# A two-layer vision tower on one core: setup and first token stage merged, first image load issued later, parameter preparations moved from VectorE to GpSimd

## The reference, cut to what matters

```python
h = tok(x, W)                                  # patches of 16 steps, real FFT, linear layer: (4, 1024, 64)
h = h + attn0(layernorm(h), wq, wkv, wo, ...)  # 16 heads, window of 128, rope, rms norm of q and k
h = h + moe0(layernorm(h), router, w1, b1, w2, b2)          # 8 experts, top 2
h = h + attn1(layernorm(h), Wq, bq, Wk, bk, Wv, bv, Wl, bl, gamma, beta)
h = h + ffn1(layernorm(h), gate_w, gate_b, w1, b1, w2, b2)  # 8 experts, top 1, limited capacity
```

## Time and profile before

| | us |
|---|---|
| median of 3 runs | 907.2 |
| lowest and highest | 906.09, 912.73 |
| profiled execution, its own time | 915.43 |
| its span in the profile | 913.3 |

### The profile page before, as it was taken

How to read it: one execution, slowest core, us unless ns; L and a number is a source line. 1 busy time by engine, 2 the same in 40 slices (tenths; PEclk the granted TensorE clock), 3 DMA queues, 4 the chain that set the end, 5 groups by cost and what they waited for, 6 DMA issues and landing times. The chain is left out here.

```text
span 913.3 us, 21178 instructions
## 1 busy us (share of the span) xinstructions
PE 734.4 (80%) x8200; PEld 481.4 (53%) x8200; DVE 611.8 (67%) x1233; ACT 449.5 (49%) x1405; POOL 411.8 (45%) x530
## 2 busy tenths in 40 slices
PE   4689999899998989988699979978899976306850
PEld 4343777435774447764277734764577753304640
DVE  0378887598885888875868836666577758504751
ACT  0022999237994359972389925212666631202000
POOL 0036666274662556643656612762033320571755
PEclk9999999999999999999979999988999987557755
DMA  8235000080000720001200000008000012117000
GB/s 294 73 137 136 2 3 3 19 247 11 3 3 1 224 50 3 4 2 27 64 2 3 3 1 1 2 2 117 1 2 3 2 53 76 36 43 121 15 11 14
DMA packets 60008, 41.30 MB, mean 45 GB/s; under 512 B 51760, under 2 KB 57389, under 8 KB 59124
## 3 DMA queue, kind: packets, MB, share of 16 engines
q1 hardware_dynamic: 57462, 33.03, 14.6%
q10 hardware_dynamic: 144, 4.19, 1.2%
q0 software_dynamic: 2304, 2.74, 0.9%
HBM read 25.44 MB, written 7.15 MB: 36 GB/s over the span
## 5 line engine op out<-in xcount | busy, mean ns | idle before, releaser
L797 ACT ACTIVATE work<-ps,small,rq 128x160 f32<-128x160 f32 x512 | 243.1, 487 | 32.7 <-DVE small L743 32.1
L776 POOL TENSOR_TENSOR work<-work,small 128x512 f32<-128x512 f32 x128 | 133.3, 1042 | 124.2 <-DVE small L760 124.2
L740 DVE TENSOR_REDUCE ps<-ps 128x4 f32<-128x640 f32 x128 | 106.6, 832 | 42.6 <-PE ps L650 41.0
L797 ACT ACTIVATION_READ_ACCUMULATOR work<-ps,small,rq 128x1 f32 x512 | 105.2, 205 | 0.0
L650 PE MATMUL ps<-kT,big 64*128 64x160 f32 x1024 | 99.1, 314 | 0.0
L752 DVE COPY pT<-ps 128x640 f32<-128x640 f32 x116 | 95.6, 824 | 0.3 <-issue 0.3
L685 PE MATMUL ps<-pT,vwin 128*64 128x128 f32 x1024 | 84.6, 283 | 9.9 <-ACT big L785 2.4
L270 PE MATMUL ps<-xT,s_proj_w 64*128 64x512 f32 x288 | 77.2, 653 | 12.1 <-PEq L213 7.0
L610 POOL TENSOR_TENSOR big<-prod 128x1024 f32<-128x1024 f32 x28 | 65.8, 2363 | 25.8 <-DVE prod L577 25.7
L650 PEld LDWEIGHTS ps<-kT,big 64*128 64x128 f32 x1024 | 77.1, 193 | 0.1
L685 PEld LDWEIGHTS ps<-pT,vwin 128*64 128x64 f32 x1024 | 57.0, 136 | 23.8 <-issue 20.1
(11 more groups left out here) (280 smaller groups left out, 1376.1 us busy)
## 6 DMA issues: line engine op xcount, KB each, us to landing
xb<-in_x SPq DMA_DIRECT2D x3, 4096.0 KB, 13.0
xb<-in_x ACTq DMA_DIRECT2D x1, 4096.0 KB, 15.2
vrem<-hl SPq DMA_DIRECT2D x64, 64.0 KB, 2.1
sent_rows<-empty_row SPq DMA_DIRECT2D x8, 325.0 KB
s_proj_w<-in_proj_w SPq DMA_DIRECT2D x1, 1536.0 KB, 6.2
big<-sent_rows SPq DMA_DIRECT2D x5, 264.0 KB, 5.1
big<-sent_rows SPq DMA_DIRECT2D x5, 256.0 KB, 4.6
xb<-in_ffn_w SPq DMA_DIRECT2D x1, 1028.0 KB, 4.7
```

The costliest lines, as they stand in the source:

```text
L740: ch.step(v.tensor_reduce(row_max(c), ps[:, s_banks(c), 0:2 * SPAN].rearrange("p e (h k) -> p e h k", h=2), X, ALU.max))
L776: g.tensor_tensor(probs[:, c % 3, :, 0:P], probs[:, c % 3, :, 0:P], bc(small[:, c % 4, 3, :], P), ALU.mult)
L797: nc.scalar.activation(probs[:, c % 3, q, :], bank[2 * (c % 2) + e][:, SPAN * hh:SPAN * hh + SPAN], ACT.Exp, bias=small[:, c % 4, 1, q:q + ...
```

## The change

The stages `setup` and `tokens` become one. ACT waits for `tok_loaded` before it issues the image load. All preparations, and three of the memsets, go from DVE to GpSimd, each as a chained step. DVE is left with four constants, `kT` and `empty_row`, the copy of the filters, then the layernorm, and `vbias` and `wvl` last. TensorE makes filters, token products, waits for `set_ready`, turns the tokens, waits for `bvrep` (`high_done`), makes the two small products (now in bank 7), then 4 instead of 6 idle products, and turns the normed tokens. On GpSimd the operations with a scalar per partition become tensor operations with a broadcast operand: `split_bias` has 9 instructions in place of 7.

```diff
-        def split_bias(v, ch, b, parts, high, low, rest):
-            ch.step(v.tensor_copy(high, b))
-            ch.step(v.tensor_tensor(rest, b, high, ALU.subtract))
-            ch.step(v.tensor_copy(low, rest))
-            ch.step(v.tensor_tensor(rest, rest, low, ALU.subtract))
-            ch.step(v.tensor_scalar(rest, rest, part_of[:, 2:3], None, ALU.mult))
-            ch.step(v.scalar_tensor_tensor(out=rest, in0=low, scalar=part_of[:, 1:2], in1=rest, op0=ALU.mult, op1=ALU.add))
-            ch.step(v.scalar_tensor_tensor(out=parts, in0=high, scalar=part_of[:, 0:1], in1=rest, op0=ALU.mult,
-                                           op1=ALU.add))
+        def split_bias(g, ch, b, parts, high, low, rest, chosen):
+            def of_part(k):
+                return part_of[:, k:k + 1].to_broadcast([P, E * D])
+            ch.step(g.tensor_copy(high, b))
+            ch.step(g.tensor_tensor(rest, b, high, ALU.subtract))
+            ch.step(g.tensor_copy(low, rest))
+            ch.step(g.tensor_tensor(rest, rest, low, ALU.subtract))
+            ch.step(g.tensor_tensor(rest, rest, of_part(2), ALU.mult))
+            ch.step(g.tensor_tensor(chosen, low, of_part(1), ALU.mult))
+            ch.step(g.tensor_tensor(rest, rest, chosen, ALU.add))
+            ch.step(g.tensor_tensor(chosen, high, of_part(0), ALU.mult))
+            ch.step(g.tensor_tensor(parts, rest, chosen, ALU.add))
...
+            @block.gpsimd
+            def _(g):
+                ch = Chain(g, S["pool_chain"])
+                ch.step(g.memset(zeros[:], 0.0))
+                ch.step(g.memset(row_of_t[:], 0.0))
+                ch.step(g.memset(window_mask[:], 0.0))
+                g.wait_ge(S["set_ready"], 1)
+                ch.step(g.tensor_tensor(bvrep[:], zeros[0:D, :], bvcol[:].to_broadcast([D, P]), ALU.add))
+                g.sem_inc(S["high_done"], 1)
+                for half in range(2):
+                    r = slice(D * half, D * half + CHUNK)
+                    ch.step(g.tensor_copy(row_of_t[r], row_of_t_rows[r]))
+                    ch.step(g.tensor_copy(window_mask[r], window_mask_rows[r]))
+                ch.step(g.tensor_scalar(bq[:], bq[:], 1.0 / D, None, ALU.mult))
+                ch.step(g.tensor_tensor(wqk[:], qn[:], kn[:], ALU.mult))
+                ch.step(g.tensor_scalar(wqk[:], wqk[:], float(np.sqrt(D)), None, ALU.mult))
+                ch.step(g.tensor_copy(moe_w2[:], sbuf["moe_w2"]))
+                ch.step(g.tensor_tensor(both_halves[:], ident[:, 0:D], ident[:, D:P], ALU.add))
+                ch.step(g.tensor_tensor(part_of[:, 0:3], ident[:, 0:3], ident[:, D:D + 3], ALU.add))
+                ch.step(g.tensor_tensor(part_of[:, 3:4], part_of[:, 0:1], part_of[:, 1:2], ALU.add))
+                ch.step(g.tensor_tensor(part_of[:, 3:4], part_of[:, 3:4], part_of[:, 2:3], ALU.add))
+                ch.step(g.tensor_tensor(part_rows[:], zeros[:], part_of[:, 3:4].to_broadcast([P, P]), ALU.add))
...
+                room = big2[:, 6:8, :].rearrange("p a n -> p (a n)")
+                split_bias(g, ch, moe_b2_rows, moe_b2[:], room[:, 0:E * D // 2].bitcast(BF16),
+                           room[:, E * D:E * D + E * D // 2].bitcast(BF16), room[:, 2 * E * D:3 * E * D],
+                           room[:, 3 * E * D:4 * E * D])
             @block.vector
...
-                v.wait_ge(S["set_ready"], 1)
-                v.tensor_copy(moe_w2[:], sbuf["moe_w2"])
...
-                v.sem_inc(S["h_ready"], 1)
                 v.wait_ge(S["tok_done"], 1)
-                v.tensor_copy(weff[:], bank[0][:].rearrange("p (o r) -> p r o", r=STRIDE)).then_inc(S["xn_ready"], 1)
+                v.tensor_copy(weff[:], bank[0][:].rearrange("p (o r) -> p r o", r=STRIDE)).then_inc(S["low_done"], 1)
+                v.wait_ge(S["h_ready"], 1)
+                layernorm(v, ch, h_next, xn_in_order, tmp, moe, st, TILES)
+                turned_vector(v, 1)
                 v.wait_ge(S["proj_done"], 1)
-                v.tensor_tensor(vbias[:], bank[1][:, 0:D], blrow[:], ALU.add)
-                ch.step(v.tensor_copy(wvl[:], bank[1][:, D:2 * D]))
+                v.tensor_tensor(vbias[:], bank[7][:, 0:D], blrow[:], ALU.add)
+                ch.step(v.tensor_copy(wvl[:], bank[7][:, D:2 * D]))
             @block.tensor
...
-                pe.wait_ge(S["h_ready"], 1)
-                nc.tensor.matmul(bank[1][:, 0:D], bvrep[:], sbuf["wl1"][:], start=True, stop=True)
...
-                ins.then_inc(S["proj_done"], 1)
-                pe.wait_ge(S["xn_ready"], 1)
                 pe.wait_ge(S["x_loaded"], 16)
+                pe.wait_ge(S["low_done"], 1)
                 for r in range(STRIDE):
                     ins = token_products(r)
                 ins.then_inc(S["prod_done"], 1)
+                pe.wait_ge(S["set_ready"], 1)
+                pe.wait_ge(S["tokens_kept"], 1)
+                turn_halves(tokensT, 3, S["tokens_turned"])
+                pe.wait_ge(S["high_done"], 1)
+                nc.tensor.matmul(bank[7][:, 0:D], bvrep[:], sbuf["wl1"][:], start=True, stop=True)
+                for r in range(2):
+                    ins = nc.tensor.matmul(bank[7][half_rows(r), D:2 * D], sbuf["wvT1"][:], sbuf["wl1"][:], start=True,
+                                           stop=True)
+                ins.then_inc(S["proj_done"], 1)
+                idle_products(5, 4, xflat[:, 0:HALF])
+                turn_normed(pe, 1)
             @block.scalar
             def _(a):
+                a.wait_ge(S["tok_loaded"], 32)
                 load_x(nc.scalar, 0, S["x_loaded"])
                 a.wait_ge(S["prod_done"], 1)
-                nc.scalar.activation(tokensT, bank[5][:], ACT.Copy)
+                nc.scalar.activation(tokensT, bank[5][:], ACT.Copy).then_inc(S["tokens_kept"], 1)
+                a.wait_ge(S["tokens_turned"], 1)
+                keep_tokens(3)
+                turned_scalar(a, 1)
...
         stage(setup)
-        stage(tokens)
```

More of the change, by code:

```diff
@@ L332, in _ @@
                 v.memset(ones_mean[:], 1.0 / (ALLT * P))
-                v.memset(zeros[:], 0.0)
                 v.memset(kT[:], 0.0)
@@ L336, in _ @@
                 v.memset(empty_row[:, TOKEN_AT:], 1.0)
-                v.memset(row_of_t[:], 0.0)
-                v.memset(window_mask[:], 0.0)
-                v.wait_ge(S["set_ready"], 1)
-                v.tensor_copy(moe_w2[:], sbuf["moe_w2"])
[L341 to L357, removed]
-                v.sem_inc(S["h_ready"], 1)
                 v.wait_ge(S["tok_done"], 1)
-                v.tensor_copy(weff[:], bank[0][:].rearrange("p (o r) -> p r o", r=STRIDE)).then_inc(S["xn_ready"], 1)
+                v.tensor_copy(weff[:], bank[0][:].rearrange("p (o r) -> p r o", r=STRIDE)).then_inc(S["low_done"], 1)
+                v.wait_ge(S["h_ready"], 1)
+                layernorm(v, ch, h_next, xn_in_order, tmp, moe, st, TILES)
+                turned_vector(v, 1)
                 v.wait_ge(S["proj_done"], 1)
-                v.tensor_tensor(vbias[:], bank[1][:, 0:D], blrow[:], ALU.add)
-                ch.step(v.tensor_copy(wvl[:], bank[1][:, D:2 * D]))
+                v.tensor_tensor(vbias[:], bank[7][:, 0:D], blrow[:], ALU.add)
+                ch.step(v.tensor_copy(wvl[:], bank[7][:, D:2 * D]))
             @block.tensor
@@ L374, in _ @@
                 ins.then_inc(S["tok_done"], 1)
-                pe.wait_ge(S["h_ready"], 1)
-                nc.tensor.matmul(bank[1][:, 0:D], bvrep[:], sbuf["wl1"][:], start=True, stop=True)
-                for r in range(2):
-                    ins = nc.tensor.matmul(bank[1][half_rows(r), D:2 * D], sbuf["wvT1"][:], sbuf["wl1"][:], start=True,
-                                           stop=True)
-                ins.then_inc(S["proj_done"], 1)
-                pe.wait_ge(S["xn_ready"], 1)
                 pe.wait_ge(S["x_loaded"], 16)
+                pe.wait_ge(S["low_done"], 1)
                 for r in range(STRIDE):
@@ L414, in keep_tokens @@
                                  bank[at][:].rearrange("p (j w d) -> p j w d", w=2, d=D), ACT.Copy).then_inc(S["h_ready"], 1)
[L416 to L434, removed]
         PAIR_ORDER = (PAIRS, *range(PAIRS))
```

## The result

The changed kernel takes 903.83 us in the median (900.97 to 907.8, 19 runs), the kernel before 910.22 (905.09 to 914.61, 19 runs). The ratio is 0.9936, with a 95% interval of 0.9921 to 0.9952: about 5.8 us faster, where 10.8 were forecast, and just outside the range's upper end of 903.5. The profiled execution's span is 902.8 us against 913.3.

What follows compares the result with a forecast made beforehand. The kernel's start was taken as one chain, bound by loads, then the filters' copy waiting behind the preparations. Projections 11.2 us earlier (41.9 for 53.06), less 0.4 for the clock: 907.2 - 10.8 = 896.4 us, range 890.0 to 903.5.

Steps and rivals of the forecast that it cites:

- GpSimd's part: Preparations on GpSimd behind `set_ready`: 23 chained instructions taking 16.2 us, from 24.5 to 40.8, with ends of 13.5 and 21.
- B: Rival, chance 0.16: GpSimd's code or mixed-type operations cost 3 to 8 us more, end 44 to 49, gain 2.6 to 7.6.
- C: Rival, chance 0.04: slower than before, GpSimd's preparations lasting 27.4 us or more and outlasting all that is won.
- nothing in that chain changes, so it ends at 36.8: Tokens' path, turning to the end of `xT`'s copies: 7.86 us as before, from 28.9 to 36.8.
- The forecast's barrier-setter: End of the merged stage: the barrier waits for GpSimd at 40.8, against DVE at 37.3; projections at 41.9.
- rival A: Chance 0.15: the tokens' path ends the stage last, DVE at 37.3; gain 14.7 us, time 892.5.
- the image, "13.0 to 15.2 us later": Image load issued at 4.2 behind the token weights, landing at 17.2 to 19.4; products at 19.4.
- Rival D: Image lands later than the filters; each us past 19.2 delays the tokens' path, first 3.5 free under GpSimd; no chance given.
- `set_ready` at 24.5: SP's last issue, which releases the preparations on GpSimd, stays about where it was, at 24.5; bounds 18.6 and 28.5.
- `set_ready` at 28: Sign named as showing the forecast wrong: SP's last issue at 28, where 24.5 was expected.
- DVE's copy to `wvl` behind GpSimd's end: Sign named as showing the forecast wrong: DVE, expected at 37.3, ending the stage behind GpSimd, expected at 40.8.
- The clock term of 0.4: First projections: TensorE's low clock after idling from about 36.3 to 41.9 costs 0.4 us more, from 0 to 1.7.

Runs made afterwards that it cites:

- the fourth experiment: The changed kernel with GpSimd waiting for its 17 early loads (`w_loaded`) in place of `set_ready`; 901.0 us against 907.49 for the kernel before, ratio 0.9939.
- The first experiment: The changed kernel without `split_bias`, `moe_b2` set to zero; 899.52 us against 907.49 for the kernel before, ratio 0.9914.

## Why the prediction was wrong

**Right:** the hole before was the filters' copy behind the preparations, and the filters' start was bound by the image's share. It was 6.0 us of that start where the prediction had some 7. The copy's 0.69, the products and the handovers came as worked out. GpSimd's part was forecast at 16.2 us and took 44.97 - 27.84 = 17.13, some 1.2 us of it where it met DVE (L258, L259 and L264 against the fourth experiment). Casts and scalars were no surprise, so B's reason falls, and C with it. B's numbers, an end at 44 to 49 and a gain of 2.6 to 7.6, came true all the same, by the late start and not by GpSimd's own speed; that they fit is luck. The small products and idle products stayed under the layernorm.

**Wrong, first: "nothing in that chain changes, so it ends at 36.8".** The 7.86 us from the turning to the end of `xT`'s copies became 12.61. I had cited the collision of GpSimd with two-input DVE instructions, priced it for GpSimd only, at up to 1 us, and left DVE as it was. I had also counted three such steps, the 512-column ones; most of the layernorm's 8-column steps have two inputs too, and four of them cost 3.1 us. The first experiment shows 4.3 us on DVE. That path, and not GpSimd's, set the stage's end: DVE ended at 45.74, GpSimd at 44.97. The forecast's barrier-setter was wrong, and rival A's (the tokens' path last) was right in kind, with an end 8.4 us later than it gave.

**Wrong, second: the image, "13.0 to 15.2 us later".** It took 18.0, and the weights that it waits for came at 5.6 and not at 4.2, so products came at 23.59, not 19.4. Rival D named this, and said that the first 3.5 us would be free under GpSimd. They weren't: GpSimd no longer ended last, since the layernorm had grown.

**Wrong, third: `set_ready` at 24.5.** It came at 27.7, inside the bounds but near the upper one: SP's issues stood for 5.41 us at one place. Had only GpSimd's path counted, 27.8 + 17.1 + 1.3 = 46.2 would still have missed the 41.9, by 4.3 of the 5.2 us. The three errors don't simply add up, because the stage ends with the later of two paths. As an estimate from these numbers, each put alone into the prediction's sum would end the stage near 42.0 (the layernorm), 41.5 (the image) and 44.0 (`set_ready`), where 40.8 was forecast; all together gave 45.74. So `set_ready` is the largest single term, 3.2 of the 5.2 us, and the layernorm's hindrance, on top of the late image, put DVE's path last. Without the hindrance GpSimd's path would still have held the stage to about 44, by the same estimate. What would show the forecast wrong was named in it, and two of its signs came: `set_ready` at 28, and DVE's copy to `wvl` behind GpSimd's end.

**The clock term of 0.4** was 0.9. With four idle products the first rope product came 2.19 us behind the projections' start even where the layernorm took 4.7 us; with six it came at 1.24, near the 1.28 of before. In that version the fifth and sixth idle call, which the prediction let go without a price, were worth 0.95 us; in the changed kernel itself, with its longer layernorm, six weren't tried.

Sum: 10.8 forecast, less 5.2 for the projections' start (47.07 in place of 41.9), less 0.5 for the clock, is 5.1, near the 4.97 seen at the first row maximum and the 5.8 of the ratio.

## What to carry to other kernels

Before work is moved to GpSimd, look at what DVE does at the same time: a two-input SBUF instruction of DVE, however small, that starts while a GpSimd instruction runs can stand until that one ends, and here each of 0.17 us then took 0.90 to 1.12. So a chain of tiny DVE steps is a bad neighbour for long GpSimd operations. Look also for the idle time of the engine that the work is taken from: here DVE had 14 us free in the very place, 6.5 of them with the loads there, and only the order was wrong. And when a large load is to follow small ones, put it behind them in one queue: here the filters' weights came as early as with the wait (5.71 against 5.59 us), and the image landed at 16.8 us, in place of 23.6 behind a wait on a second engine.

## What the runs showed of the hardware that was not expected

- A DVE instruction of 8 columns with two SBUF inputs took 0.90 to 1.12 us beside GpSimd's 1.05 to 1.27, against 0.17 alone, and ended with GpSimd's instruction; a one-input reduction of 512 columns took 0.69 either way. The Trainium skill (GPSIMD Engine Reference, Key points) names contention with DVE instructions that have two SBUF inputs, and the trace agrees. Which side stands goes by which starts second: DVE's in these, GpSimd's L264 behind L232.
- The number of inputs isn't all: with the image as SP's third DMA, L230, a TENSOR_SCALAR with one tensor input of 8 columns, took 0.97 us in place of 0.17 and ended at 36.50, with GpSimd's L259 at 36.48.
- `MODIFY_POOL_CONFIG` ran at 2.0 us here, and GpSimd's first TENSOR_TENSOR behind the wait took 0.39 us, like the 0.40 of the shape in the earlier trace rows. The 6 us that the Trainium skill (GPSIMD Engine Reference, Instruction dispatch) gives for the first call did not show; in the changed kernel they could have been paid under the wait, but in the kernel before only 3.4 us lie between the two records and the first call.
- GpSimd was slowed as well, by less in sum: 1.48 against 1.15 us for the same subtraction (L259), 0.95 against 0.61 for the cast L258 and 1.79 against 1.27 for L264, in the changed kernel against the version that waits for its own loads.
- The image landed 18.0 us after ACT's issue at 5.57. As SP's third DMA it landed 15.3 us after its issue at 1.54, before the filters were copied. What makes its way 2.7 us longer in the first case, descriptors ahead of it or its packets between small ones, wasn't tried.
